# Self-attention steps with all four maxima and exponentials ahead of the step's copies, values' restore and share products

## The reference, cut to what matters

```
# L0: 16 heads of 16, causal
att = einsum('bhqd,bhkd->bhqk', q, k) * scale;  att = where(causal, att, -inf)
y = einsum('bhqk,bhkd->bhqd', softmax(att), v)
# L3, first attention: 16 heads of 32
a = softmax(einsum('bhsd,bhtd->bhst', q, k) * D ** -0.5)
a = a * (arange(t)[None, :] > arange(s)[:, None])     # mask after the softmax
o = einsum('bhst,bhtd->bhsd', a, v)
```

## Time and profile before

| | |
|---|---|
| median of three runs | 3064.89 us (3061.54 to 3069.56) |
| profiled execution, its own time | 3065.05 us |
| its span in the profile | 3063.3 us |
| mean granted TensorE clock | 0.898 of full speed |
| busy: PE, PEld, DVE, ACT, POOL | 2480.4, 1646.6, 1309.0, 889.6, 690.2 us |
| transfers | 57 GB/s over the span |

### The profile page before, as it was taken

One profiled execution on the slowest core, in us unless ns is written; L12 is line 12 of the kernel. 1 busy time (PEld: TensorE's weight loads), 2 busy tenths in 40 slices (PEclk: granted clock), 3 DMA queues, 4 the chain that ended last, 5 costly groups with the idle time before them and its releaser, 6 DMA issues.

```text
span 3063.3 us, 32462 instructions
## 1 busy us (share of the span) xinstructions
PE 2480.4 (81%) x11538; PEld 1646.6 (54%) x11538; DVE 1309.0 (43%) x2768; ACT 889.6 (29%) x1970; POOL 690.2 (23%) x767
## 2 busy tenths in 40 slices
PE   4888978879487619997489988989988667999995
PEld 2444644546346517775144555544555435888873
DVE  5555245553544421112475453465443542333324
ACT  0635235542242102221164422364422110111110
POOL 3421231222100040002301032110032054222236
PEclk7999989999698659998699999999988678999998
DMA  9000000000002032221000000000000033555533
GB/s 358 16 1 1 1 1 1 1 1 1 14 0 111 0 123 92 90 93 47 26 1 1 1 1 1 0 1 1 1 1 1 1 134 129 194 197 204 195 133 116
DMA packets 65152, 175.15 MB, mean 57 GB/s; under 512 B 6656, under 2 KB 45696, under 8 KB 56832
## 3 DMA queue, kind: packets, MB, share of 16 engines
q0 software_dynamic: 21504, 96.49, 9.1%
q1 hardware_dynamic: 43536, 77.18, 7.1%
HBM read 123.18 MB, written 50.46 MB: 57 GB/s over the span
## 4 chain that ended last, share of the span: by engine, by line
PE 62%; DVE 13%; issue 11%; POOL 9%; ACT 3%; DMA 1%; SPq 0%; DVEq 0%; POOLq 0%; ACTq 0%
PE PS L1943 8%; PE PS L553 6%; PE PS L953 5%; PE PS L944 5%; PE PS L1728 5%; PE PS L1742 5%; PE PS L1955 4%; PE PS L583 4%; PE PS L494 3%; PE PS L903 3%; PE PS L533 2%; POOL slots L2043 2%; POOL arena L2057 2%; PE PS L743 2%; DVE arena L657 2%
## 5 line engine op out<-in xcount | busy, mean ns | idle before, releaser
L614 ACT ACTIVATE arena<-PS,arena 128x512 f32<-128x512 f32 (+3 forms) x512 | 305.4, 605 | 215.4 <-DVE arena L657 201.7
L553 PE MATMUL PS<-arena 64*128 64x512 f32 (+3 forms) x1024 | 296.5, 566 | 53.4 <-ACT arena L614 42.6
L657 DVE TENSOR_REDUCE arena<-PS 128x1 f32<-128x512 f32 (+3 forms) x512 | 272.5, 581 | 33.5 <-PE PS L559 24.9
L274 POOL TENSOR_TENSOR arena<-arena 128x4 f32<-128x4 f32 x53 | 55.6, 1050 | 938.1 <-DVE arena L285 375.4
L1943 PE MATMUL PS<-arena 128*128 128x256 f32 (+1 forms) x1152 | 260.3, 382 | 0.9 <-DVE arena L1979 0.9
L1943 PEld LDWEIGHTS PS<-arena 128*128 128x128 f32 (+1 forms) x1152 | 210.1, 182 | 42.1 <-issue 1.3
L837 POOL TENSOR_TENSOR arena<-arena 128x512 f32<-128x512 f32 x144 | 118.2, 825 | 434.5 <-ACT arena L810 427.0
L553 PEld LDWEIGHTS PS<-arena 64*128 64x128 f32 x1024 | 102.4, 186 | 168.3 <-ACT arena L614 115.6
L583 PE MATMUL PS<-arena 128*128 128x128 f32 x1280 | 178.9, 289 | 15.5 <-ACT arena L614 15.5
L583 PEld LDWEIGHTS PS<-arena 128*128 128x128 f32 x1280 | 147.2, 148 | 68.9 <-ACT arena L614 50.1
L944 PE MATMUL PS<-arena 128*128 128x512 f32 x384 | 168.3, 594 | 3.1 <-ACT arena L961 3.1
(11 more groups left out here) (333 smaller groups left out, 3972.1 us busy)
## 6 DMA issues: line engine op xcount, KB each, us to landing
arena<-e SPq DMA_DIRECT2D x8, 2048.0 KB, 8.5
arena<-slots SPq DMA_DIRECT2D x56, 256.0 KB, 3.4
yslots<-arena POOLq DMA_DIRECT2D x56, 256.0 KB, 2.6
slots<-zeros SPq DMA_DIRECT2D x1, 12288.0 KB, 40.5
slots<-zeros SPq DMA_DIRECT2D x1, 5120.0 KB, 35.9
arena<-w3a SPq DMA_DIRECT2D x1, 4106.0 KB, 13.1
arena<-w3b SPq DMA_DIRECT2D x1, 3593.0 KB, 21.1
arena<-slots SPq DMA_DIRECT2D x8, 384.0 KB, 8.8
```

Of the source, the lines that this page charges most:

```text
L553: ins = nc.tensor.matmul(PS[:, hh, 0:w], q[:, t * P:(t + 1) * P], k[:, 0:w], start=True, stop=not cfg["causal"])
L614: nc.scalar.activation(PRB[m % 6][:, 0:w], PS[:, hh, 0:w], ACT.Exp, bias=nmax[:, m:m + 1], accum_out=rsum[:, col:col + 1]).then_inc(s["pro ...
L657: nc.vector.tensor_reduce(nmax[:, m:m + 1], PS[:, hh, 0:w], AX, ALU.max, negate=True).then_inc(s["nmax"], 1)
```

## The change

In both loops the split into two halves goes. ScalarE does the four exponentials of the round, then `raw` of step n-3, then both its block columns of step n-1. VectorE does the four maxima, then `shared_out` of step n-3, then all its block columns of step n-1. TensorE's list, every wait, every instruction and the number of buffers stay the same.

```
@@ act_self
             for n in range(NSTEPS + 1):
-                for half in range(2):
-                    if n < NSTEPS:
-                        exp(n, 2 * half)
-                        exp(n, 2 * half + 1)
-                    if half == 0 and n >= 3:
-                        raw(n - 3)
-                    if n >= 1:
-                        turn(n - 1, half, 1)
+                for hh in range(4) if n < NSTEPS else ():
+                    exp(n, hh)
+                if n >= 3:
+                    raw(n - 3)
+                if n >= 1:
+                    turn(n - 1, 0, 2)
@@ dve_self
                 if n < NSTEPS:
                     top(n, 0)
                     top(n, 1)
+                    top(n, 2)
+                    top(n, 3)
                 if n >= 3:
                     shared_out(n - 3)
-                if n >= 1:
-                    turn(n - 1, 0, 1)
-                if n < NSTEPS:
-                    top(n, 2)
-                    top(n, 3)
                 if n == 0:
                     dve_project(v, s, it, cfg, "v")
                 if n >= 1:
-                    turn(n - 1, 1, 3)
+                    turn(n - 1, 0, 4)
```

## The result

Five runs of the changed kernel gave 3043.62 to 3048.34 us, median 3044.55; five of the kernel before, on the same footing, 3061.54 to 3070.28, median 3065.81. The ratio is 0.993 with a 95% interval of 0.9916 to 0.9943: faster by 0.7%, 21 us by the medians, where 14.7 had been forecast. The profiled execution took 3044.51 us (span 3042.8), 20.5 us less than that of before. The mean granted TensorE clock went from 0.898 to 0.901.

The account below looks back on a forecast made before the run. Passes were taken as bound by TensorE's list and the waits in it. L3's -5.3 and L0's -9.4 gave -14.7 us on 3065.05, so 3050.2 against 3064.89; eight-in-ten range 3037 to 3067.

Parts of the forecast that it names:

- `raw` late: L3, round 4: `raw` behind the fourth exponential delays share product and maxima, so the first exponential comes 1.71 us later.
- whole L3 group: L3, third exponential of round 1 to the next: 20.68 us becomes 21.14, 0.46 longer.
- L0: L0's four passes: opening -2.0, groups -0.43 and +0.5, last group -0.4; -2.3 us a pass, -9.4 together.
- TensorE doesn't feel most of this: L3, round 4: TensorE turns three columns meanwhile, covering most of the first exponential's 1.71 us delay.
- The values' first part: Each group: it waits for ScalarE's last copy, now behind the fourth exponential, and starts 0.59 us later in L3.
- L3's opening: Start of each L3 pass: maxima no longer stand behind a copy; 2.15 us shorter, at most 2.8.
- Round 2's third exponential: L3's opening: it comes 0.77 us behind the column instead of 1.92, the maxima being done long before.
- the 21.6 that the prediction named as a sign of being wrong: L3's groups: the prediction is wrong if they are over 21.6 or under 20.7 us apart.
- The clock: TensorE's low-clock spells in the passes: left unchanged in the sum; a mean granted clock moving over 0.005 would refute the prediction.
- the first (spells go): Rival for the openings: shorter gaps remove four low-clock spells of 2.6 us, 10 us on top, 3040; chance 0.13 not given, 0.12.
- The prediction's own example: Low-clock spell at 1664 to 1668 us, granted 0.50, said to follow a TensorE wait on VectorE; cost 2.6 us.
- The slower rival: Round 4 of 12 L3 and 4 L0 groups: `raw` wait uncovered, 1.71 us each, net +10.8, 3076; chance 0.13.

Follow-up runs that it names:

- e1: Only VectorE's order changed against the kernel before (four maxima ahead of share product and copies), ScalarE's loop left old; 3022.35 us, ratio 0.986.
- e2: Only ScalarE's order changed against the kernel before (four exponentials, then both copies), `raw` left behind the second exponential; 3074.87 us, ratio 1.0025.
- e8: New order in each pass's first four rounds only, the kernel before's order from the fifth on; 3047.09 us, ratio 0.9937.
- e3: The changed kernel with `raw` put back behind the second exponential; 3020.79 us, ratio 0.9856.
- e7: The change in L0's four passes alone, L3's keeping the order of the kernel before; 3054.98 us, ratio 0.9965.
- e4: The changed kernel with the old order of both engines in rounds that turn four columns; 3027.79 us, ratio 0.9883.
- e9: e5 with both of ScalarE's copies ahead of the third exponential where four columns are turned; 2989.54 us, ratio 0.9752.
- e5: e3 and e4 together on the changed kernel; 3012.36 us, ratio 0.9826.
- e6: The change in L3's four passes alone, L0's keeping the order of the kernel before; 3050.19 us, ratio 0.9962.

## Why the prediction was right, and where it was off

The mechanism holds in every step that the runs took apart. Openings get shorter since VectorE's maxima no longer stand behind a copy that waits for TensorE: e1 has the gain, e2 has at most 0.3 us of it, e8 has it with nothing else changed. `raw` late holds the share product, that the maxima of round 4, and through VectorE's unbroken list the fourth column: e3. ScalarE's second copy late holds the values: e4. The net of a whole L3 group, +0.46 forecast and +0.48 measured, is the sum of such terms with both signs.

That the passes' sum at full clock came out so near, -14.3 for -14.7, is in part luck: L3 gave -3.6 where -5.3 was forecast and L0 -10.7 where it was -9.4, and the two misses cancel. (Four times L0's terms, -2.33 each, is -9.3; the prediction has -9.4.)

One sentence of the walk misleads, "TensorE doesn't feel most of this", of the 1.71 us by which round 4's first exponential is late. It is true against the old order, in which round 4's third exponential came no earlier (0.18 later in the walk). Against the new order with `raw` early, TensorE feels 1.64 of it (e3).

Sizes, step by step:
- **The values' first part**, forecast 0.59 later, came 0.5 later (1.98 to 2.47 behind the third exponential): two copies in a row follow at 0.5 us, not 0.60. The same 0.09 shows in e2.
- **L3's opening**, forecast -2.15, was -1.67 and -1.94. The step that was mis-sized is "Round 2's third exponential ... comes behind the column and maxima that are done long before: 0.77". In the changed kernel:

```profile
1637.11 0.66 PE L583 MATMUL PS<-arena 128*128 128x128 f32 x4
```

```profile
1636.35 2.48 DVE L655 TENSOR_REDUCE arena<-PS 128x1 f32<-128x512 f32 x4 [0.36 <-PE PS L553]
```

```profile
1637.08 0.69 ACT L614 ACTIVATE arena<-PS,arena 128x512 f32<-128x512 f32 x1 [6.23 <-DVE arena L655]
...
1638.42 0.69 ACT L614 ACTIVATE arena<-PS,arena 128x512 f32<-128x512 f32 x1
```

  These are the timelines of TensorE, VectorE and ScalarE in L3's second pass. The four scores come in one go, as nothing holds them in the second step; so the maxima are not done but run one behind another from 1636.35, ScalarE's four exponentials follow at 0.67 from 1637.08, and the third is at 1638.42, 1.31 behind the column's start (1637.11; 1.24 from the 1637.18 at which the chain of waits, from which the prediction read its columns, would have it) and not 0.77. e8 bears it out: there the fourth column doesn't wait for the late copy, and the opening gains 2.33 us where the walk had 2.8 without that wait. So the sign of round 2's third exponential, right behind the column and released by TensorE, didn't hold in L3's openings.
- **L3's second group in passes 1 and 3**, +0.75: I had priced it like the others. What sets it apart is the normalisation's second part, which stands there on VectorE; that this makes the difference was not tried. These groups are now 22.2 us, above the 21.6 that the prediction named as a sign of being wrong; they were at 21.46 before, which it hadn't looked at.
- **L0**, forecast -9.4 and measured -10.7 at full clock: the opening of the first pass gained 0.28 more than I took over from L3's walk, the others' 0.14 less, and the group without a share product and the last one 0.15 and 0.19 more.
- **The clock**: "In my sum the spells stay as they are." They did not: -9.8 us in L3, +4.2 in L0. This step carries most of what the sum missed (5.6 of the profile's 5.8 us, 20.5 against 14.7).

Of the rivals, the first (spells go) came half true. It gave the openings as the reason, and for L3's openings the eleven traces agree: where they had the old order (before, e2, e7) 8 of 12 held a spell, and where VectorE had the new one (all other kernels) 1 of 32. The Trainium skill ("TensorE: Matmul & The Clock Gate", "HAM oscillation — how this bites in real kernels") has the rule that gaps in the matrix engine's work bring the slow clock. L3's openings agree with it: TensorE's waits in them got shorter (longest 1.59 to 1.29 us in passes 1 and 3, 1.15 to 0.84 in the others). L0's openings disagree: their longest wait fell from 0.45 to 0.18 us in passes 2 to 4, and they have more spells. The prediction's own example is read a little off: the wait ahead of its spell was for ScalarE's exponential (1.15 us, ended at 1659.13), which had waited for VectorE's maximum.

Where L0's new spells sit can be read from the eleven traces, one execution each, though no run was made to test it. The changed kernel's clock in two of them (windows: busy times, then granted clock):

```profile
132.50:135.50 3.00, 3.00 (x16) 2.77 (x16) 1.46 (x5) 0.93 (x5) 0.00 (x0) 0.50 0.00 0
576.20:579.40 3.20, 3.20 (x17) 3.20 (x16) 1.52 (x4) 0.61 (x4) 3.12 (x3) 0.50 0.00 0
```

The first is in a group with a share product. Such groups hold a spell in 6 of the 12 L0 passes of the three kernels with `raw` late there (the changed kernel, e4, e7) and in none of the 32 of the other eight: these spells go with the late `raw`. The second, 16 to 18 us into an opening, has its like in 6 of the 32 openings with VectorE's new order and in none of the 12 with the old. A third kind starts with a pass's first exponential, in 4 of 12 openings in the old order and 11 of 32 in the new: it doesn't go with the order. What brings the second kind, behind waits of at most 0.18 us, stays open.

The slower rival had the right wait and the right place, but the wrong cover: the 1.71 us of `raw` reached the path as 1.64 a group in e3's comparison (1.04 to 1.64 over its 16 places), yet the changed order without it wins 1.2 us a group (20.68 to 19.52 in e3, 19.46 in e1). The price of a wait has to be set against the same group's other terms, which the forecast did and the rival did not.

## What to carry to other kernels

Group the instructions of an engine by who waits for their result, not by kind: a wait at the head of a list (here the share product's for `raw`) holds everything behind it. For each of the two engines ask separately what the next engine is short of: maxima first on VectorE was worth 1.4%, while on ScalarE the copies and `raw` were the short ones, and putting both copies ahead of two exponentials (e9) was worth as much again as the whole change (0.9826 to 0.9752). A walk through one period with the trace's own durations gave L3's group length in seven kernels (the changed kernel, e1 to e5, e9) within 0.15 us, which is far finer than the whole run can tell.

## What the runs showed of the hardware that I had not expected

- The granted clock of a stretch goes with the order of instructions on other engines: L3's first two passes in the old order were granted 0.96 and 0.94 in each of two executions (the third 0.98 and 0.96, the fourth 0.98 and 1.00), all four 1.00 in the new order in two. The second group of L3's passes 1 and 3 held a spell in all 8 cases of e4, e5, e8 and e9, behind a TensorE wait of 1.7 to 2.9 us, and in none of the 8 of the changed kernel, e1, e3 and e6.
- The length of TensorE's longest wait doesn't tell where a spell comes. The changed kernel, e3 and e6 have a wait of 1.51 us in every L3 group behind the opening, at clock 1.00 throughout; in L3's second pass before, a spell at about 1662 us followed a wait of 1.15 us, and in L0's fourth pass after, the one at 576 us came with no wait over 0.2 us since the pass's first exponential.
- Two heads' scores of 512 on different halves of the array's rows take 1.06 us when they start together and 1.73 when their exponentials release them 0.67 apart (1700.27 and 1700.93 in the kernel before): the second then ends 0.67 later, and nothing of it is made up.
- The kernel before spread over 0.4% in one set of 20 runs (3059.7 to 3073.0), in two bunches: 12 runs up to 3062.2 at a mean granted clock of 0.898 to 0.900, 8 from 3068.3 at 0.895 to 0.897. e9 had 4 of 5 within 0.06%; e6 shows two bunches as well (six at 3050 to 3052, three from 3058 to 3062).
